# A decoder layer with cross-attention on one core: the same units of work in another written order

## The reference

```python
def xattn(Q, K, V, Wq, bq, Wk, bk, Wv, bv, Wo, bo):      # Q (16,64,256), K = V = context (16,1601,256)
    q, k, v = proj(Q, Wq, bq), proj(K, Wk, bk), proj(V, Wv, bv)
    scores = jnp.einsum('bhqd,bhkd->bhqk', q, k) / jnp.sqrt(jnp.float32(16))
    attn = jax.nn.softmax(scores, axis=-1)
    ctx = jnp.einsum('bhqk,bhkd->bhqd', attn, v)
    return ctx.transpose(0, 2, 1, 3).reshape(16, 64, 256) @ Wo.T + bo

x = x + xattn(layernorm(x), ctx, ctx, ...)               # almost all of the time
x = x + self_attention(layernorm(x), ...)                # rotary, 16 heads, 64 keys
x = x + experts(layernorm(x), ...)                       # top-1 of 8, capacity 128
```

## Time and profile before

| | before |
|---|---|
| median of 3 runs | 706.86 us (705.21 to 708.08) |
| the profiled execution's own time | 707.65 us |
| its span, first to last instruction | 705.8 us |
| TensorE matmul busy | 668.2 us (95%) |
| VectorE busy | 561.4 us (80%) |
| GpSimd busy | 552.8 us (78%) |
| ScalarE busy | 454.3 us (64%) |
| mean granted TensorE clock | 0.995 |

### The profile page before, as it was taken

How to read it: one execution, slowest core, us unless ns; L and a number is a source line. 1 busy time by engine, 2 the same in 40 slices (tenths; PEclk the granted TensorE clock), 3 DMA queues, 4 the chain that set the end, 5 groups by cost and what they waited for, 6 DMA issues and landing times.

```text
span 705.8 us, 21770 instructions
## 1 busy us (share of the span) xinstructions
PE 668.2 (95%) x8632; PEld 500.2 (71%) x8681; DVE 561.4 (80%) x1138; ACT 454.3 (64%) x901; POOL 552.8 (78%) x376
## 2 busy tenths in 40 slices
...
GB/s 309 109 250 213 30 124 172 92 154 82 149 110 150 105 171 94 160 102 173 90 169 86 179 96 166 84 182 88 172 89 106 99 150 2 3 1 8 92 65 93
DMA packets 45691, 84.21 MB, mean 119 GB/s; under 512 B 8684, under 2 KB 28436, under 8 KB 45588
## 3 DMA queue, kind: packets, MB, share of 16 engines
...
## 4 chain that ended last, share of the span: by engine, by line
PE 71%; DVE 8%; DMA 6%; POOL 4%; issue 4%; ACT 4%; SPq 3%; ACTq 0%; POOLq 0%; DVEq 0%
PE ps_kv L825 14%; PE ps_kv L834 14%; PE ps_score L885 11%; PE ps_front L857 10%; PE ps_out L906 9%; DMA cbuf<-in_ctxT 2%; SPq L512 2%; POOL prob L650 2%; PE ps_score L930 2%; DMA kstack<-khigh 2%; DVE maxes L1531 1%; PE ps_out L922 1%; ACT prob L1252 1%; PE ps_kv L796 1%; PE ps_front L930 1%
## 5 line engine op out<-in xcount | busy, mean ns | idle before, releaser
L650 POOL TENSOR_TENSOR prob<-prob 128x1024 bf16<-128x1024 f32 (+1 forms) x198 | 374.8, 1912 | 64.0 <-ACT prob L1252 62.5
L1531 DVE TENSOR_REDUCE maxes<-ps_front 128x1 f32<-128x512 f32 (+1 forms) x416 | 265.7, 664 | 52.0 <-PE ps_front L857 49.6
L1252 ACT ACTIVATE prob<-ps_score 128x512 f32<-128x512 f32 (+1 forms) x416 | 236.1, 597 | 71.8 <-PE ps_score L885 63.2
L885 PE MATMUL ps_score<-qstack,kstack 98*128 98x128 bf16 (+1 forms) x1664 | 152.1, 219 | 2.3 <-ACT prob L1252 1.6
L857 PE MATMUL ps_front<-kstack,qstack 96*128 96x512 bf16 (+1 forms) x512 | 145.9, 334 | 5.7 <-DVE maxes L1531 3.0
L885 PEld LDWEIGHTS ps_score<-qstack,kstack 98*128 98x128 bf16 (+1 forms) x1664 | 113.0, 99 | 36.1 <-ACT prob L1252 4.7
L906 PE MATMUL ps_out<-vstack,prob 128*128 128x33 bf16 (+1 forms) x3328 | 129.3, 178 | 4.8 <-DVE oparts L1557 3.5
L906 PEld LDWEIGHTS ps_out<-vstack,prob 128*128 128x128 bf16 (+1 forms) x3328 | 117.3, 97 | 20.8 <-issue 3.7
L834 PE MATMUL ps_kv<-w_hi,cbuf 128*128 128x256 bf16 (+1 forms) x402 | 109.8, 273 | 0.9 <-DVE vstack L1521 0.9
L834 PE MATMUL ps_kv<-w_hi,clow 128*128 128x256 bf16 (+1 forms) x402 | 109.4, 272 | 0.0
L834 PE MATMUL ps_kv<-w_lo,cbuf 128*128 128x256 bf16 (+1 forms) x402 | 109.4, 272 | 0.0
...
## 6 DMA issues: line engine op xcount, KB each, us to landing
kstack<-khigh SPq DMA_DIRECT2D x256, 100.1 KB, 2.2
...
kstack<-klow SPq DMA_DIRECT2D x128, 100.1 KB, 2.2
qstack<-q_blocks SPq DMA_DIRECT2D x48, 64.0 KB, 2.4
...
```

What stands on the lines that cost most here:

```text
L650: nc.gpsimd.tensor_tensor(p_parts(slot, 1)[0:n], prob[slot][0:n, :, 0, :], p_parts(slot, 0)[0:n], ALU.subtract).then_inc(plow_gps, 1)
L885: mm = nc.tensor.matmul(ps_score[0:nn, h % NSB, j * P:(j + 1) * P], kstack[par][0:98, hp, n0:n0 + nn], qstack[par][0:98, q_at(hp), :], sta ...
L1252: nc.scalar.activation(prob[slot][0:nn, HP * e:HP * e + HP, 0, :], ps_score[0:nn, h % NSB, :].rearrange("p (h q) -> p h q", h=HP), ACT.Exp)\
L1531: nc.vector.reduce_max(maxes[:, hp:hp + len(unit), n], ps[:, 0:len(unit) * nn].rearrange("p (h k) -> p h k", k=nn), AX.X).then_inc(m_free, 1)
```

## The change

The letters of the four strings stand in another order, from the first batches up to the end of the last batch (the letter `Z`); from there on the strings are the same. Each letter is there as often as before, so each engine issues the same instructions, and no other line of the program differs. One line of each string as an example:

```diff
 PE_PROGRAM = [
-     "wssmKsmswmwswmsmKsmsmwwsmswmwsmsKmwmsswmKmwwwswswwwswsKmmsswwmKsmswwKmssmKwwmssmwwmKmmsKmmswKmmssKwm"
+     "wmmKmsmswwwmswsmKsmswmwswmswmwwsmsmKsmmswwKmwwswwswwssKsmsmwswKsmsmwKwssmmKmssmwwwmKmmKmmwsKmssmKmsw"
...
 ACT_PROGRAM = [
-     "KeKeeeKeKKeeRKRKeeeeKeeDKeeKeKeeeKeeeKeeKeeKeeeKKeeKReKeKRKeeeKeKeeeDKeKeeKKeeeKeKeeKeeKeeeegeeKeKeR"
+     "KeKeeKeeKKReeKRKeeKeeDeeKeeKeeKeeKeeeKeeKeeKeKeeKeeKReKKeReeKeKeKDeeKeeKeeKKeeKeeeKKeeeeKeeegeeKKeeR"
...
 POOL_PROGRAM = [
-    ("qcvccvvfqcfvvcvcvfccppppppppppppppppppccppcpcppppcpqppppfcpppcppcppppccpcppfpcpppppppppcppppppcppcpc"
+    ("qcvccvvfqcfvvccvcvcfpppppppppppppcpppppcpcpppcqpppcpppcppppcppcppfppcpcpcppppppfpppcppppcppppppcppcp"
...
```

More of the change, by code:

```diff
@@ L110 @@
 PE_PROGRAM = [
-    ("KKKKKKKKKKKKKmmKmmKmKmKmmKmKmKmmKmKmmmKKmmKmKmmKmKmmKKmmKmKmmsKmsmsKmsmsKmwsmswmwsKsmswmwwmKmsswmKwm"
-     "wssmKsmswmwswmsmKsmsmwwsmswmwsmsKmwmsswmKmwwwswswwwswsKmmsswwmKsmswwKmssmKwwmssmwwmKmmsKmmswKmmssKwm"
[L113 to L125, removed]
@@ new lines @@
+    ("KKKKKKKKKKKKKmmKmmKmKmKmmKmKmKmmKmKmmmKKmmKmKmmKmKmmKKmmKmKmmsKmsmsKmsmsKmswsmwmsKsmsmKmwwssmwwwmKss"
+     "wmmKmsmswwwmswsmKsmswmwswmswmwwsmsmKsmmswwKmwwswwswwssKsmsmwswKsmsmwKwssmmKmssmwwwmKmmKmmwsKmssmKmsw"
+     "wwsmwwmKswsmmwwsKmsmwKmssmKmsmsKwwwmwKswmKsKmssmwwwsmwsmKsmmsKwwswsmwKmswsmKswmsmKmwwmwswwsmmwsKmssm"
+     "KmwmwsKsmwsmKmssmwwwmKmsmKmKswswwmwwwKsKwssmmKmmswsmKmssKmswwwsKwmmwKwsmwsKmsmsKswmKmwsmwswwmwsKsmsm"
+     "KmwsmswwwmwsmsKwsmmwsKmwmKmKwwmwsKwwsKssKsKsmmsKmmsswwwwsmmKsmwmwsKwwmsmswKswmmswKmsswmKsmwsmwwwsmKm"
+     "smswKmmwsKmmsKmswwmKmmwwwwKwwsmKssKssKmmsKswmwsmKmsmwswKwmsmwsKKmmsKmsswwmwswmKsmmKmwswsmKsmswmwwKsm"
+     "wswmwsKmmsKmmsKmmwwwwwKwmsKsswwKssmmKsmKmsswwwwmsmsKsmsmwwwsKmwswmwsmKmsKmssKmmswwwwwmsmKmmwwsKmswKm"
+     "smKsmmKmwwssKmwmwKwsmKssKmswwswmmsKsmsmKwwswwmsKmswKsmwmKswmwwsmsKmwsmKmsmKwsmwswmKswmKmwswmwwmssKmm"
+     "sKmmssKmmKwwwwwmsKswswwKssKsmmwsKmswsmwwsmwsmKmsmwsKwmwwmsKmswmsKsmwsmKswmmKmswsmwKsmKmwsmswmwwmKmsm"
+     "sKmmwKwwwwmswKwswsKssmmKsmsmwKsmwwwmssKsswmKwwwsmKsmKmwwsmwsmKmswwwsmmKsmsmKmsmKswwmswwsKmmsKmKmmKmm"
+     "wwwKwsswmwKssKswwsKsmmKsmwsmwwswmsmKwsmswmwKswmsKmswmKmwmKssmmKmswwsmwwmswKmssmKmsmwKwmmsKwmsKwswwmm"
+     "wKwmKssKwssmwwmssKmsmswwwwmmssKmswKsmwswmKswmKmmsKwsmswKsmsmKmwsmwKwmwmKwwmswmwsKmmsKmmsKmmsKwwswwms"
+     "wKsKswwwsKmmssKwsmwsmKmsswmwwmsKswmwsmKmswmwswmwsmKsmmKwmssmwKmmssKwmwmswKmsKsmmKmsswKwwmmwKwsmKwwws"
+     "wwsmmsKmsmsKmssKmswwsmwmwwKswwsmmsKsmmswKwmswswwmKsmsmwKmsmswKmsmwKmKwmmssKmswsKwmwwmKmKmwsKmmsswwww"
+     "wsmsKmsmsKsmwmwKsswmmwwswsmKmmsKmsmwwsmKmsmwswwmwsmwsmswmKwsmsmKwsmmswswmmsZmwswwsAwswwwwssOswsAwsww"
@@ L129 @@
 ACT_PROGRAM = [
-    ("KKgKKKKKKKKKKKKKKgKKKKKKKKKKKKRKKReKeeeeKeKeeKeeKeeeeeeKKeeeeeeKeeReeKReeDeKeKeeKeeKeeKeKeeKeKeeeege"
-     "KeKeeeKeKKeeRKRKeeeeKeeDKeeKeKeeeKeeeKeeKeeKeeeKKeeKReKeKRKeeeKeKeeeDKeKeeKKeeeKeKeeKeeKeeeegeeKeKeR"
[L132 to L136, removed]
+    ("KKgKKKKKKKKKKKKKKgKKKKKKKKKKKKRKKReKeeKeeeeKeKeeKeeKeeeeKeeeeKeeeeeeRRKeeDeeKeeKeeKeKeeKeKKeeKeeeege"
+     "KeKeeKeeKKReeKRKeeKeeDeeKeeKeeKeeKeeeKeeKeeKeKeeKeeKReKKeReeKeKeKDeeKeeKeeKKeeKeeeKKeeeeKeeegeeKKeeR"
+     "KKRKDeeKeeKeeKeeeeKKeeKeeeKeeeKeKeeKeKeeKeeKKRKDeRKeeKeeKeeKeKeeKeKeKeKeeKeeKeeegeKeeeKKeKReKReKeDeK"
+     "eeeKeeKeeeKeeKeeKeeKKeeeKeeKKeKeKeKReKReKeeKeeDeeKeKeeKeeKeKeKeeKeKeeegKeeKeeKeeKKRReKeDeKeeeKeeeeKe"
+     "KeKeeeKeeKeeKKeKeeKeeKeeKRKReKeDeKeeKeeeKeeKeeKeKeeKeeKeeKeKeegeKKKeeRKeeKReKeKDeeeKeeKeeKeeKeKeKeee"
+     "KKeeeKeKeKeeKKeReKRKeeeeDeeKKeeeeKeKeKeeKeKeeKeKeegKeeKKeeKReKeeRKeKDeeKeeKeeKeeeKeeeKeeeKeKeKeKeKee"
+     "KeKKeReeRKeKeeDKeeeeKeeKKeeeeKeeeKeeKKeeKKeKeeKKeReKRKeKeeDeeeKeeKKeeeeKeeKeeKeeeeZKeeeKeReeReeeAeDe"
      "eeeAeeeeeeeeeeeeeHeeeHeeBATVTBVEEPPHEDEVA2PTPBAH2EEPfPHViBTV2ABTEEfPPifEEPi2PAHlAV2HBTffHiTiBElVEVPT"
```

20 lines of the change are left out of this document (10 added, 10 removed).

## The result

The kernel after took 696.07 us (median of four runs, 695.15 to 696.66), beside 707.02 us for the kernel before on the same chip (four runs, 705.21 to 708.08): a ratio of 0.985, 95% interval 0.982 to 0.987. The forecast was 700.6 us. The profiled execution took 695.15 us (span 693.3), that of before 707.65 (span 705.8), so the traces have 12.5 us between them to explain, a little more than the medians' 11.0.

The account below looks back on a forecast made before the run. TensorE, with matmuls over 95% of the span, was taken as the bound, with only its idle time to win. −6.2 − 1.7 + 1.6 = −6.3 us from the 706.86 us median gave 700.6 us, range 694.5 to 709.0.

Parts of the forecast that it names:

- Part 1: Batch ends on ScalarE and VectorE: TensorE's waits for maxima, scaling and exponentials shrink, −6.2 us (ends 0 and 8.2).
- three quarters: Share taken of the 8.2 us of batch-end waits, as three waits lie elsewhere and one place stays short: −6.2 us.
- The count: TensorE's work at 14 batch ends against 2.7 us needed (3.3 behind an exponential): four places short before, one now.
- Part 2: Clock drop at 167.40 to 171.00 us, following the removed 1.39 us wait, goes: −1.7 us (ends 0 and −1.7).
- Part 3: GpSimd's context subtract ahead of the last chunk at three batch ends: +1.6 us (ends −0.9 and +5.4).
- I take the row of 2.03 us: Assumed transfer wait of GpSimd's moved context subtracts, costing 2.5 us, less the old 0.9 us wait.
- Part 4: Transfers and the rest: waits for keys (1.5 us in two) unchanged, 0, ±1.5; from Z on 0, ±1.
- From Z on nothing is moved.: Stretch from letter Z (about 578 us) on: counted as 0, ends ±1 for the other engines' progress at Z.
- all of it goes: Rival: batch-end waits 8.2, clock 1.7 and GpSimd's wait 0.9 us vanish with nothing new: 696.1 us, chance 0.12.
- GpSimd takes it back: Rival, no change: busy GpSimd can't follow, so TensorE waits for chunks instead of maxima: 706.7 us, chance 0.25.

Follow-up runs that it names:

- The late copies in the new order: The changed kernel with ScalarE's copy of ps_out moved back behind the next batch's exponentials at five batch ends: 714.11 us, ratio to before 1.0109.

## Why the prediction was right in kind and 4.5 us short

- **Part 1, −6.2 forecast.** Measured by its own rule: the 5.6 us in 16 waits became 0.2 in one, so −(5.4 + 15 × 0.16) = −7.8 us. The step that failed is "three quarters", a share that I took between bounds and not from a row. The count itself showed every place but one clear of 2.7 us, and that one short by 0.07; it could have been believed. The late copies in the new order, at 12.5 us where the count gave 11, bear it out.
- **Part 2, −1.7.** The drop near 167 us is gone: −1.7 between these two executions. That it hung on the removed wait was less certain than I wrote. With GpSimd's new string in the kernel before, the same unit waits as long (1.38 us), and no drop follows; with VectorE's and GpSimd's new strings it waits 1.39 us, and none follows either. These runs agree with the rule of the Trainium skill that I weighed against it ("TensorE: Matmul & The Clock Gate", section "What's actually happening": the chip watches in its own rhythm). Over executions the clock gave less: its mean is 0.997 in the four after and 0.996 in the 57 of the kernel before beside the experiments, which makes some 0.7 us and not 1.7.
- **Part 3, +1.6.** Measured −0.9: the old wait for GpSimd went, and no new one came. The failed step is the price: "I take the row of 2.03 us". These were waits at other batch ends, in an order in which the transfer was late. At none of the three new places did the subtract wait, and putting it back changed nothing.
- **Part 4, 0.** Waits for keys fell from 1.5 us in two to 0.7 in three: 0.8 − 0.16, so −0.6 us, within its ±1.5.
- **"From Z on nothing is moved."** True of the letters behind `Z`, but a pair just ahead of it moved, and its instructions run behind it: −1.4 us. The failed step is the count of nothing for `Z`: I had priced the moved letters only where TensorE waited in the front.

Together −7.8 − 1.7 − 0.9 − 0.6 − 1.4 = −12.4 us, of the 12.5 between the profiled executions. The first four make −11.0, where the front by its own ends gave −10.6, and the 0.5 us ahead of the first `m` is in none of them. The medians differ by 11.0. Of the 1.5 us between, about 1 us is the choice of execution: the two profiled ones differ by a clock drop of 1.7 us, all executions by 0.7 on average. What is left is within the 2 to 5 us over which most kernels' runs here spread.

The rival "all of it goes" (chance 0.12) is what happened. That its 696.1 us meets the 696.07 so closely is luck: it has nothing for the keys and for the pair ahead of `Z`, 2.0 us together, and it counts the whole clock drop. "GpSimd takes it back" failed although GpSimd is as busy as before (106.97 of 112 us): its letters had moved along with TensorE's, and with its old string TensorE waits 5.1 us for its chunks.

What stays open: why GpSimd's old string costs the new kernel 7 us and its new string the old kernel only 1.8. Part of it is the pair ahead of `Z`, which the old string loses and the new one saves. Without its 1.3 us the order in the front costs the new kernel some 6 us and the old one some 3. In the new kernel the trace has most of that: 5.1 us of waits for chunks in seven, 7 × 0.16 under the rows, and a clock drop of 1.7 near 138 us, of the 7.0 us by which the front is longer there, with 1.2 us of waits for keys gone. For the difference between 6 and 3 I have no count.
